# Loading the first batch's rows ahead of the first modulation weights in an AdaLN transformer layer, with zeros multiplied in the meantime

## The chip, the cores and the metric

The kernel runs on one core of a Trainium2 chip, as one program launched once. Its time is in device microseconds (us), from several executions. The profile is a record of one such execution, which has its own time.

The engines named below are PE (TensorE, matrix multiplication, with a separate row PEld for its weight loads), DVE (VectorE), ACT (ScalarE), POOL (GpSimd) and SP (SyncE, which issues most DMA transfers). SPq is SP's sequencer, on which a DMA issue takes time.

## The reference

One layer with adaptive layer norm over four batches of 512 tokens, 512 wide, all in float32:

```
mod = (silu(c) @ wmod).reshape(4, 6, 1, -1)      # c: 4 x 512, wmod: 512 x 3072
sa, ca, ga, sb, cb, gb = (mod[:, 0], ..., mod[:, 5])
ga, gb = sign-preserving max(|g|, 0.25) of each
h = layernorm(x) * (1 + ca) + sa
x = x + ga * attention(h, Wq, bq, Wk, bk, Wv, bv, Wo, bo)     # 16 heads of 128, causal
h = layernorm(x) * (1 + cb) + sb
x = x + gb * ffn(h)        # softmax router, top 2 of 8 experts, and shared experts
```

The change touches only the beginning: the first two pieces of `mod` (`sa`, called piece 0, and `ca`, called piece 1), each a product of the 4 x 512 matrix silu(c) with 512 x 512 weights, and the layer norm of the first batch's rows, which are multiplied by 1 + ca and have sa added.

## The kernel before, in words

The program is written engine by engine: each engine has its own list of instructions, run in the order written, and the lists are tied together by semaphores. No planner moves anything. Three stages follow one another: stage 1 (normalised rows, transposed; the q and k projections of all heads), stage 2 (values, scores, softmax, output projection) and stage 3 (router, experts, result). Matrix products of the stages are made of three products each, of high and low parts (`h_hi`, `h_lo` and so on), so that they keep float32 accuracy.

The very first part of stage 1 is what matters here.

- SP issues its transfers one after another on one queue (L621 to L650): `c_in`; piece 0 of the modulation weights, 1 MB, into `stage[0]` (L631, issued by the helper at L624); the four tiles of the first batch's rows, 256 KB each, into `x_in` (L633), each with its own semaphore; piece 1 of the weights into `stage[1]` (L634); five small constants, the identity and the causal mask among them (L635 to L639); the first quarter of Wq into `stage[2]` (L640); pieces 3 and 2 of the weights into `mod_early` (L641, L642); the second batch's rows (L643). Then it waits for piece 0's product (`mod_full` 1, L644) and issues raw weights and the rows of batches 2 and 3.
- `stage[0..2]` and `x_in` all are parts of the large tile `acc`, so the profile writes `acc<-wmod`, `acc<-x` and `acc<-wq` for these loads.
- ACT computes silu(c) (L1249), copies the products of pieces 0 and 1 out of PSUM into slots 2 and 3 of the tile `q_out` (L1252), and later scales transposed rows (`hidden`, L1262) and rounds them to their high part (`high`, L1269).
- PE waits for silu(c), then runs `mod_piece` (L1585 to L1592) for piece 0 and piece 1. A piece is four matmul calls over chunks of 128 rows, c = 0 to 3, with silu(c) (128 x 4) as the stationary operand and 128 x 512 weights moving. All are float32; one call appears as two MATMUL records. Then PE waits for the constants (L1607), transposes the first tile of normalised rows (L1608, in the helper at L1602), transposes the modulation rows (L1612), transposes the other three tiles, runs pieces 3 and 2 (L1617, L1618), and starts the projections of batch 0, `plain(0)` (L1626 to L1633, matmuls at L1577).
- DVE takes statistics of the four tiles as they land (`stats(0)`, L2019), POOL makes a seed for the inverse root (L952), DVE refines it and normalises the tiles (L2031 to L2036). DVE then waits for the transposed modulation rows (L2088), puts them into `modc` (L2091), scales tile 0 of the transposed rows (L2046), makes Wq's low part (L2096) and the rows' low parts (`h_low`, L2053, `hlo_ok`), and goes on with the statistics of the second batch.
- POOL rounds the first quarter of Wq (L969) as soon as it has landed.

Of the kernel before, what the change touches and what calls it, by code (L numbers as in the profile page):

```python
# [30 lines left out]
P = 128  # L31
D = 512
# [182 lines left out]
def adaln_layer(nc, x, wq, bq, wk, bk, wv, bv, wo, bo, gate_t, wexp, c_t, wmod, ident_in, causal_in,  # L215
                tri_in, coef_in, out):
    ctx = ExitStack()
    with ctx:
        def sem(name):
            return ctx.enter_context(nc.semaphore(name))  # L220

        def sbuf(scope, name, shape, dt=F32):
            return scope.enter_context(nc.sbuf_tensor(name, shape, dt))
# [15 lines left out]
        bank = [ctx.enter_context(nc.psum_tensor(f"bank{i}", [P, T], F32)) for i in range(8)]  # L239
# [22 lines left out]
        def chunks(at, dims, **sizes):  # L262
            width = int(np.prod(list(sizes.values())))
            return acc_cols[:, at:at + width].rearrange(f"p ({dims}) -> p {dims}", **sizes)

        stage = [chunks(s * DC * D, "c n", c=DC, n=D) for s in range(3)]
# [37 lines left out]
        q_out = sbuf(s1, "q_out", [P, 4, T])  # L304
# [122 lines left out]

        const_ld = sem("const_ld")
        c_ld = sem("c_ld")
        modw_ld = {0: sem("modw_ld0"), 1: sem("modw_ld1"), 3: sem("modw_ld_later"), 2: sem("modw_ld2")}  # L430
        modw_ld[4] = modw_ld[5] = modw_ld[3]
        wq0_ld = sem("wq0_ld")
        raw_ld = [sem("raw_ld0"), sem("raw_ld1")]
        x0_ld = [sem(f"x0_ld{i}") for i in range(TT)]
# [1 line left out]
        wq0_hi_ok = sem("wq0_hi_ok")  # L436
        wq0_ok = sem("wq0_ok")

        silu_c = sem("silu_c")
        mod_full = sem("mod_full")  # L440
        mod_ev = sem("mod_ev")
# [150 lines left out]
        wmod_v = wmod.rearrange("(c p) n -> p c n", p=P)  # L592
# [26 lines left out]
        def _(sp):  # L619
# [3 lines left out]
            def mod_weights(m, to):  # L623
                sp.dma_start(to, wmod_v[:, :, m * D:(m + 1) * D]).then_inc(modw_ld[m], 16)  # L624
# [3 lines left out]
                sp.dma_start(raw[i % 2], (wq_v if kind == "q" else wk_v)[:, :, pair * 2 * P:(pair + 1) * 2 * P])\  # L628
                  .then_inc(raw_ld[i % 2], 16)

            mod_weights(0, stage[0])  # L631
            for t in range(TT):
                sp.dma_start(x_in[:, t, :], x_t[:, t, :]).then_inc(x0_ld[t], 16)  # L633
            mod_weights(1, stage[1])  # L634
            sp.dma_start(ident[:, :], ident_in).then_inc(const_ld, 16)  # L635
            sp.dma_start(causal[:, :], causal_in).then_inc(const_ld, 16)
            sp.dma_start(bq_c[:, :], bq).then_inc(const_ld, 16)
# [933 lines left out]
        def _(pe):  # L1571
            def mm3(dst, terms):
# [5 lines left out]
                        k += 1  # L1578
                return ins

            pe.wait_ge(silu_c, 1)

            MOD_FREE = {3: (mod_ev, 1), 2: (modc_ok, 2), 5: reader(0, 1), 4: (s_exp, 3)}

            def mod_piece(m, w, to):  # L1585

                pe.wait_ge(modw_ld[m], {5: 32, 4: 48}.get(m, 16))
                if m in MOD_FREE:
                    pe.wait_ge(*MOD_FREE[m])
                for c in range(DC):  # L1590
                    ins = pe.matmul(bank[to][0:B, :], c_silu[:, c, :], w[:, c, :], start=(c == 0), stop=(c == DC - 1))
                ins.then_inc(mod_full, 1)  # L1592

            def transposes(b, i):
# [8 lines left out]
                ins.then_inc(tx_full, 1)  # L1603

            mod_piece(0, stage[0], 6)
            mod_piece(1, stage[1], 0)
            pe.wait_ge(const_ld, 5 * 16)  # L1607
            transposes(0, 0)  # L1608
# [6 lines left out]
            for i in range(1, TT):  # L1615
                transposes(0, i)
            mod_piece(3, mod_early[:, 0], 6)  # L1617
            mod_piece(2, mod_early[:, 1], 7)  # L1618

# [363 lines left out]
            for n in range(Z0 + 1, NJ):  # L1983
                k = n - Z0
# [6 lines left out]
        def _(dve):  # L1991
# [3 lines left out]
            def link(ins):  # L1995

                dc[0] += 1
                ins.then_inc(dchain, 1)
                dve.wait_ge(dchain, dc[0])
# [12 lines left out]
            def stats(b):  # L2012

                if b:
                    dve.wait_ge(x_ld[b - 1], 16)
                for i in range(TT):
                    if b == 0:
                        dve.wait_ge(x0_ld[i], 16)
                    ins = dve.bn_stats(stat[:, i, :], xs[b][:, i, :])  # L2019
                link(ins)  # L2020
                for i in range(TT):
                    ins = dve.bn_aggr(ln_mv[:, b, i, :], stat[:, i, :])
                link(ins)
                dve.tensor_scalar(ln_ve[:, b, :], ln_mv[:, b, :, 1], EPS, None, ALU.add).then_inc(ln_var, 1)

            def normalise(b):

                dve.wait_ge(ln_var, b + 1)
                dve.wait_ge(ln_seed, b + 1)
                seed = ln_rs0[:, b, :]  # L2030
                link(dve.tensor_tensor(nt1[:, :], seed, seed, ALU.mult))  # L2031
                link(dve.tensor_tensor(nt2[:, :], nt1[:, :], ln_ve[:, b, :], ALU.mult))
                link(dve.tensor_scalar(nt1[:, :], nt2[:, :], -0.5, 1.5, ALU.mult, ALU.add))
                link(dve.tensor_tensor(rstd[:, :], nt1[:, :], seed, ALU.mult))
                for i in range(TT):
                    dve.tensor_scalar(xs[b][:, i, :], xs[b][:, i, :], ln_mv[:, b, i, 0:1], rstd[:, i:i + 1],  # L2036
                                      ALU.subtract, ALU.mult).then_inc(xn_ok, 1)
# [43 lines left out]
            def sums_low(i):  # L2081
                s = (i + 1) % 2
                dve.wait_ge(uh_ok, 2 * i + 2)
                dve.tensor_tensor(s_w[1][s], s_raw, s_w[0][s].bitcast(F32), ALU.subtract).then_inc(ul_ok, 1)

            stats(0)
            normalise(0)
            dve.wait_ge(modt_full, 1)  # L2088
# [549 lines left out]
            for n in range(Z0, NJ - 1):  # L2638
                k = n - Z0
# [66 lines left out]
```

## Time and profile before

| what | value |
| --- | --- |
| median of 3 executions | 1536.74 us (1535.05 to 1537.42) |
| profiled execution, its own time | 1537.87 us |
| span of its record | 1535.7 us |
| mean granted TensorE clock | 0.998 |
| PE busy | 1507.5 us, 98% of the span |
| DVE, ACT, POOL busy | 988.1, 734.4, 717.1 us |
| share of PE in the chain that ended last | 86% |
| DMA | 304.05 MB, mean 198 GB/s |

The busy times are sums over the instructions of an engine, and an engine's share is its busy time over the span. The chain that ended last is followed back from the last instruction, at each step to what released it. The span is cut into 40 equal slices on the page, 38.4 us each: PE is at 7 tenths in the first slice, at 9 in all between and at 8 in the last.

### The profile page before, as it was taken

To read this page: it belongs to the slowest core of one execution; us is meant where nothing else is said; L and a number is where in the kernel's file an instruction comes from. 1 tells how busy PE (TensorE), PEld (TensorE's weight loads), DVE (VectorE), ACT (ScalarE), POOL (GpSimd) and SP (SyncE) were. 2 spreads that over 40 slices of the span, in tenths; PEclk is the share of its full clock that TensorE was granted. 3 is DMA by queue.
4 is the path that set the end of the run, shared out by engine and by line. 5 is a ranking of instruction groups with operands and counts; after the bars stand their busy time and mean duration, and the time that the engine had idled before them with its cause. 6 is when DMAs were issued, how large, how long until landed. Compare 5 with 4: busy or idle time off the path is not lost.

```text
span 1535.7 us, 29335 instructions
## 1 busy us (share of the span) xinstructions
PE 1507.5 (98%) x8844; PEld 1344.4 (88%) x8844; DVE 988.1 (64%) x2222; ACT 734.4 (48%) x1743; POOL 717.1 (47%) x767
## 2 busy tenths in 40 slices
PE   7999999999999999999999999999999999999998
PEld 3688888887999999999999999988999899999997
DVE  5977666677777777777777777774458322222268
ACT  3542222345666666666666666663332233333333
POOL 1212433346765566666566656678823211111054
PEclk9999999999999999999999999999999999999999
DMA  9336555577858486656757484745243455755566
GB/s 319 124 135 209 209 195 192 187 264 248 258 163 247 148 251 185 204 179 208 213 174 233 140 249 144 238 146 204 79 167 144 179 200 199 279 222 206 188 192 197
DMA packets 203295, 304.05 MB, mean 198 GB/s; under 512 B 80384, under 2 KB 142208, under 8 KB 196048
## 3 DMA queue, kind: packets, MB, share of 16 engines
q1 hardware_dynamic: 196096, 281.80, 54.8%
q0 software_dynamic: 5680, 18.62, 4.1%
q10 hardware_dynamic: 1440, 2.62, 0.5%
q8 instruction: 45, 0.74, 0.2%
q14 instruction: 34, 0.28, 0.1%
HBM read 187.35 MB, written 115.64 MB: 197 GB/s over the span
## 4 chain that ended last, share of the span: by engine, by line
PE 86%; DVE 4%; POOL 3%; DMA 3%; issue 2%; ACT 1%; SPq 0%; POOLq 0%; ACTq 0%; DVEq 0%
PE bank L1577 47%; PE bank L1675 17%; PE bank L1790 7%; PE bank L1742 7%; PE bank L1773 4%; PE bank L1844 2%; PE bank L1880 1%; DMA xin<-ffn_rows,slot_tokens 1%; DMA keys<-k_ring 1%; DMA ffn_rows<-h 1%; DMA acc<-wq 1%; POOL acc L1023 0%; POOL acc L1021 0%; DVE h L2629 0%; DVE h L2614 0%
## 5 line engine op out<-in xcount | busy, mean ns | idle before, releaser
L1577 PE MATMUL bank<-w,xt_hi 128*128 (+2 forms) x1136 | 281.5, 330 | 1.1 <-DMA w<-experts_lo 1.0
L1577 PEld LDWEIGHTS bank<-w,xt_hi 128*128 128x128 f32 x1136 | 196.8, 189 | 7.9 <-DMA w<-experts_lo 1.3
L1577 PE MATMUL bank<-w,xt_lo 128*128 (+2 forms) x568 | 183.6, 323 | 0.0
L1401 ACT ACTIVATE prob<-prob,row_inv 128x128 f32<-128x128 f32 (+3 forms) x256 | 137.4, 560 | 79.6 <-DVE row_inv L2243 79.4
L2363 DVE TENSOR_TENSOR ht_lo<-bank,ht_hi 128x128 fp32r<-128x128 f32 (+1 forms) x213 | 48.4, 283 | 181.7 <-ACT ht_hi L1518 181.6
L1389 ACT ACTIVATE prob<-bank,neg_max 128x128 f32<-128x128 f32 (+3 forms) x256 | 133.8, 526 | 41.3 <-DVE neg_max L2235 41.1
L1577 PE MATMUL bank<-wv_hi,h_hi 128*128 128x256 f32 x512 | 147.1, 287 | 0.0
L1577 PE MATMUL bank<-w,ht_hi 128*128 (+3 forms) x426 | 140.1, 410 | 5.2 <-DVE ht_lo L2363 4.5
L1577 PE MATMUL bank<-wv_lo,h_hi 128*128 128x256 f32 x512 | 144.7, 283 | 0.0
L1577 PE MATMUL bank<-wv_hi,h_lo 128*128 128x256 f32 x512 | 144.7, 283 | 0.0
L1201 POOL DMA_INDIRECT xin<-ffn_rows,slot_tokens x39 | 39.8, 1022 | 185.8 <-PE bank L1844 181.5
L2230 DVE TENSOR_REDUCE row_max<-bank 128x1 f32<-128x128 f32 (+3 forms) x256 | 119.8, 489 | 6.6
L986 POOL TENSOR_TENSOR ch_lo<-ch_raw,ch_hi 128x340 fp32r<-128x340 f32 x128 | 117.8, 921 | 10.3
L984 POOL CAST q_hi<-q_raw 128x512 fp32r<-128x512 f32 x62 | 69.0, 1112 | 114.9 <-PE bank L1742 109.0
L1000 POOL TENSOR_TENSOR k_ring<-acc,k_ring 128x512 fp32r<-128x512 f32 x48 | 62.1, 1307 | 120.8 <-ACT k_ring L1371 120.8
L2206 DVE TENSOR_TENSOR pt_lo<-bank,pt_hi 128x512 fp32r<-128x512 f32 (+1 forms) x192 | 106.3, 596 | 5.4 <-ACT pt_hi L1415 2.5
L1577 PEld LDWEIGHTS bank<-w,xt_lo 128*128 128x128 f32 x568 | 106.8, 188 | 0.0
L1491 ACT ACTIVATE xt_hi<-bank 128x512 fp32r<-128x512 f32 x71 | 42.5, 599 | 132.3 <-PE bank L1844 132.3
L2206 DVE TENSOR_TENSOR v_lo<-bank,v_hi 128x512 fp32r<-128x512 f32 x64 | 44.3, 692 | 94.3 <-ACT v_hi L1408 94.3
L1675 PE MATMUL bank<-t_parts,unit_hi 128*128 128x512 f32 x336 | 103.5, 389 | 0.0
L986 POOL TENSOR_TENSOR q_lo<-q_raw,q_hi 128x512 fp32r<-128x512 f32 x62 | 97.5, 1573 | 5.0
L1577 PEld LDWEIGHTS bank<-wv_lo,h_hi 128*128 128x128 f32 x512 | 97.7, 191 | 0.1
(249 smaller groups left out, 4125.8 us busy)
## 6 DMA issues: line engine op xcount, KB each, us to landing
keys<-k_ring SPq DMA_DIRECT2D x64, 512.0 KB, 3.5
ch_raw<-wexp SPq DMA_DIRECT2D x128, 170.0 KB, 3.0
experts_hi<-ch_hi SPq DMA_DIRECT2D x128, 170.0 KB, 2.6
experts_lo<-ch_lo SPq DMA_DIRECT2D x128, 170.0 KB, 2.7
w<-experts_hi SPq DMA_DIRECT2D x10, 2176.0 KB, 7.9
w<-experts_lo SPq DMA_DIRECT2D x10, 2176.0 KB, 14.6
q_transposed<-q_out SPq DMA_DIRECT2D x64, 256.0 KB, 2.1
k_even<-keys SPq DMA_DIRECT2D x16, 1024.0 KB, 5.5
```

What stands on the lines that cost most here:

```text
L984: pool.tensor_copy(hi, raw).then_inc(split_hi, 1)
L986: pool.tensor_tensor(lo, raw, hi.bitcast(F32), ALU.subtract).then_inc(done, 1)
L1000: pool.tensor_tensor(ring[e][:, 1, :], src, ring[e][:, 0, :].bitcast(F32), ALU.subtract).then_inc(kl_ok, 1)
L1389: ins = act.activation(prob[:, h, ROW_AT[r]:ROW_AT[r] + (r + 1) * P], bank[s_bank(i, first and m is n)][:, at:at + (r + 1) * P], ACT.Exp, ...
L1401: ins = act.activation(part, part, ACT.Copy, scale=row_inv[:, h, r:r + 1])
L1577: ins = pe.matmul(dst, a, m, start=(k == 0), stop=(k == last))
L1675: ins = pe.matmul(bank[to[j]][:, :], a, m, start=q == 0, stop=q == 5)
L1742: ins = pe.matmul(dst, a[:, h, r * P:w], k_both[s][:, key, h, 0:w], start=(k == 0), stop=(k == 2))
L1773: ins = pe.transpose(bank[PT_BANKS[g]][:, at + (r - k) * P:at + (r - k + 1) * P], prob[:, h, ROW_AT[r] + k * P:ROW_AT[r] + (k + 1) * P], i ...
L1790: ins = pe.matmul(bank[6 + h][:, k * P:T], a[:, k, vals], m[:, h, cols], start=(k == 0 and q == 0), stop=(g == 2 and q == 2))
L2206: dve.tensor_tensor(dst, src, hi.bitcast(F32), ALU.subtract).then_inc(done, 1)
L2230: ins = dve.tensor_reduce(row_max[:, h, r:r + 1], at_bank[:, at:at + (r + 1) * P], AX_X, ALU.max)
```

## The change

SP issues the four row tiles first, then piece 0 of the modulation weights, then piece 1 as two transfers of 512 KB, each with a semaphore of its own: chunks 0 and 1, and chunks 2 and 3. PE waits for the two halves separately, inside the loop over chunks. At its start DVE fills slot 0 of `q_out` with zeros, and PE, as its first work, multiplies those zeros by themselves four times into PSUM bank 5, whose content is not used. Slot 0 of `q_out` and bank 5 are written anew by their usual producers later.

```
-        modw_ld = {0: sem("modw_ld0"), 1: sem("modw_ld1"), 3: sem("modw_ld_later"), 2: sem("modw_ld2")}
+        modw_ld = {0: sem("modw_ld0"), 3: sem("modw_ld_later"), 2: sem("modw_ld2")}
         modw_ld[4] = modw_ld[5] = modw_ld[3]
+        mod1_ld = [sem("modw_ld1_first"), sem("modw_ld1_rest")]
...
+        idle_ok = sem("idle_tile_ok")
...
-            mod_weights(0, stage[0])
             for t in range(TT):
                 sp.dma_start(x_in[:, t, :], x_t[:, t, :]).then_inc(x0_ld[t], 16)
-            mod_weights(1, stage[1])
+            mod_weights(0, stage[0])
+            for k in range(2):
+                sp.dma_start(stage[1][:, 2 * k:2 * k + 2, :], wmod_v[:, 2 * k:2 * k + 2, D:2 * D]).then_inc(mod1_ld[k], 16)
...
+            pe.wait_ge(idle_ok, 1)
+            for _ in range(4):
+                pe.matmul(bank[5][:, :], q_out[:, 0, 0:P], q_out[:, 0, :], start=True, stop=True)
             pe.wait_ge(silu_c, 1)
...
             def mod_piece(m, w, to):
 
-                pe.wait_ge(modw_ld[m], {5: 32, 4: 48}.get(m, 16))
+                if m != 1:
+                    pe.wait_ge(modw_ld[m], {5: 32, 4: 48}.get(m, 16))
                 if m in MOD_FREE:
                     pe.wait_ge(*MOD_FREE[m])
                 for c in range(DC):
+                    if m == 1 and c % 2 == 0:
+                        pe.wait_ge(mod1_ld[c // 2], 16)
                     ins = pe.matmul(bank[to][0:B, :], c_silu[:, c, :], w[:, c, :], start=(c == 0), stop=(c == DC - 1))
                 ins.then_inc(mod_full, 1)
...
+            dve.memset(q_out[:, 0, :], 0.0).then_inc(idle_ok, 1)
             stats(0)
             normalise(0)
```

## Rows read from the trace of the kernel before

**Rows 1.** The page: engines' busy time, and the chain that ended last.

```profile
PE 1507.5 (98%) x8844; PEld 1344.4 (88%) x8844; DVE 988.1 (64%) x2222; ACT 734.4 (48%) x1743; POOL 717.1 (47%) x767
PE 86%; DVE 4%; POOL 3%; DMA 3%; issue 2%; ACT 1%; SPq 0%; POOLq 0%; ACTq 0%; DVEq 0%
```

**Rows 2.** Timeline of PE: start, length, instruction, count, idle before with its releaser.

```profile
6.71 9.43 PE L1591 MATMUL bank<-acc,c_silu 128*4 128x512 f32 x16 [6.71 <-DMA acc<-wmod]
16.06 0.66 PE L1602 MATMUL bank<-ident,acc 128*128 128x128 f32 x4
...
17.23 1.53 PE L1602 MATMUL bank<-ident,acc 128*128 128x128 f32 x12
18.69 7.03 PE L1591 MATMUL bank<-mod_early,c_silu 128*4 128x512 f32 x16
25.65 0.50 PE L1577 MATMUL bank<-h_hi,unit_hi 128*128 128x512 f32 x1
```

**Rows 3.** Timeline of PEld in the same stretch, the weight loads of pieces 0 and 1.

```profile
7.51 0.13 PEld L1591 LDWEIGHTS bank<-acc,c_silu 128*4 128x4 f32 x1 [0.72 <-issue]
8.37 0.13 PEld L1591 LDWEIGHTS bank<-acc,c_silu 128*4 128x4 f32 x1 [0.72 <-issue]
...
12.54 0.09 PEld L1591 LDWEIGHTS bank<-acc,c_silu 128*4 128x4 f32 x1 [0.34 <-issue]
...
15.11 0.09 PEld L1591 LDWEIGHTS bank<-acc,c_silu 128*4 128x4 f32 x1 [0.34 <-issue]
```

**Rows 4.** DMA issues at 1.22, 3.48, 4.01 and 7.08 us: count, size, us to landing.

```profile
acc<-wmod SPq DMA_DIRECT2D x1, 1024.0 KB, 5.3
...
acc<-x SPq DMA_DIRECT2D x2, 256.0 KB, 5.8
...
acc<-wmod SPq DMA_DIRECT2D x1, 1024.0 KB, 8.1
...
acc<-wq SPq DMA_DIRECT2D x1, 1024.0 KB, 8.3
```

**Rows 5.** Timeline of SP's issues at the start.

```profile
1.22 0.50 SPq L624 DMA_DIRECT2D acc<-wmod  x1
1.77 2.20 SPq L633 DMA_DIRECT2D acc<-x  x4
4.01 0.45 SPq L624 DMA_DIRECT2D acc<-wmod  x1
```

**Rows 6.** Windows: us, busy of PE, PEld, DVE, ACT, POOL, PEclk, DMA share, GB/s.

```profile
3.00:4.00 1.00, 0.00 (x0) 0.00 (x0) 0.00 (x0) 0.00 (x0) 0.00 (x0) 1.00 0.75 233
7.00:8.00 1.00, 1.00 (x2) 0.13 (x1) 0.70 (x2) 0.00 (x0) 0.00 (x0) 1.00 1.07 410
9.00:10.00 1.00, 1.00 (x2) 0.13 (x1) 1.00 (x2) 0.00 (x0) 0.00 (x0) 1.00 1.05 389
```

**Rows 7.** Timeline of DVE, ACT and POOL around the same work.

```profile
7.30 2.73 DVE L2019 BATCH_NORM_STATS2 stat<-acc 128x6 f32<-128x512 f32 x4 [7.30 <-DMA acc<-x]
12.76 1.92 DVE L2036 TENSOR_SCALAR acc<-acc,ln_mean_var,rstd 128x512 f32<-128x512 f32 x4
15.45 1.90 POOL L969 CAST unit_hi<-acc 128x2048 fp32r<-128x2048 f32 x1 [3.61 <-DMA acc<-wq]
16.17 0.59 ACT L1252 ACTIVATE q_out<-bank 4x512 f32<-4x512 f32 x1 [2.85 <-PE bank L1591]
17.34 0.26 DVE L2091 TENSOR_SCALAR modc<-bank 128x16 f32<-128x16 f32 x2 [2.67 <-PE bank L1612]
23.88 1.29 DVE L2053 TENSOR_TENSOR h_lo<-h_raw,h_hi 128x512 fp32r<-128x512 f32 x2 [1.22 <-ACT h_hi L1269]
```

**Rows 8.** First instructions of POOL, and a later fill by POOL.

```profile
0.72 0.10 POOL L946 MEMSET minus_half<- 128x4 f32 x1 [0.29 <-POOLq L2699]
L1136 POOL MEMSET ones<- 128x128 f32 x1 | 0.2, 206 | 0.0
```

**Rows 9.** Timeline of PE around its longest later gaps.

```profile
75.48 1.98 PE L1602 MATMUL bank<-ident,x_later 128*128 128x128 f32 x16 [1.66 <-issue]
77.53 0.39 PE L1577 MATMUL bank<-h_lo,unit_hi 128*128 128x512 f32 x1
77.77 0.39 PE L1577 MATMUL bank<-h_hi,unit_lo 128*128 128x512 f32 x1
...
1048.10 0.66 PE L1844 MATMUL bank<-ident,xin 128*128 128x128 f32 x4 [1.98 <-DMA xin<-ffn_rows]
```

## The prediction

> **What bounds the kernel now.** I read the page first. PE is busy for 98% of the span and carries 86% of the chain that ended last [rows 1]. So an edit pays only where PE stands still or runs slowly, or where it moves work off PE. The one place in the record where PE stands still for long is the start: PE's timeline shows nothing before 6.71 us, released by the first transfer of modulation weights [rows 2]. Its other gaps are at most 1.98 us [rows 9].
>
> The next view is the weight loads of that first block. There are 16 MATMUL records for the eight calls of pieces 0 and 1. The loads come 0.86 us apart at first (7.51, 8.37) and 0.43 us apart later (12.54 to 15.11 is six steps of 0.43) [rows 3]. Instruction and shape are the same, so PE ran at half speed, 1.2 GHz, after having stood idle, and rose to 2.4 GHz while it worked. The granted clock in the windows reads 1.00 in both parts [rows 6]; here the spacing tells more than that column. The last load stands at 15.11 and its matmul begins one step later, so the block ends at 15.11 + 0.43 + 0.43 = 15.96, and the transposes begin at 16.06. Of n half-speed records, 0.853n + 0.427(16 - n) = 15.96 - 6.71 = 9.25 gives n = 5.7, or 4.85 us at half speed. The slow start costs 5.7 x 0.427 = 2.4 us.
>
> The third view is the transfers. Piece 0 landed at 1.22 + 5.3 = 6.52, the fourth row tile at 3.48 + 5.8 = 9.28, piece 1 at 4.01 + 8.1 = 12.11, Wq's quarter at 7.08 + 8.3 = 15.38 [rows 4]. 1 MB takes 2.8 us between landings, and the DMA engines are full from 4 us on, at 389 to 410 GB/s [rows 6]. So in this stretch the landing time of a transfer is set by the bytes ahead of it and hardly by the moment of its issue.
>
> What follows the block is one chain: ACT's copy at 16.17, `modc` at 17.34 [rows 7], the transposes to 18.76, pieces 3 and 2 from 18.69 (16 x 0.427 = 6.83, to 25.5), the projections at 25.65 [rows 2]. The last low part of the rows, which the projections need too, ends at 23.88 + 1.29 = 25.17 [rows 7], 0.4 us before PE is free; it hangs on `modc` as well. Whatever moves the end of piece 1 moves all of this equally.
>
> **The change part by part.**
>
> *Rows first.* Piece 0 now has 1 MB of rows ahead of it. Together they are the 2 MB that had landed at 9.28 before, so I put piece 0's landing at 9.28. Bounds: it is issued at 1.22 + 2.20 + 0.05 = 3.47 [rows 5], and from there the nearest rows are 5.3 us (nothing ahead) and 8.1 us (two other MB ahead) [rows 4], which is 8.8 to 11.6. The value by bytes lies near the low end, as it should, since by 3.47 only part of one MB is still ahead. PE started 0.19 us after the landing, so 9.47 instead of 6.71: a loss of 2.76 us if nothing else changed.
>
> *Zeros.* DVE's fill has nothing before it; POOL's first instructions run at 0.72. POOL fills 128x128 in 0.21 us [rows 8], DVE passes 128x512 in 1.92 / 4, near 0.5 us [rows 7]; the fill is between these and 0.85, and I take 0.5, so PE begins at 1.3. Four float32 calls are eight records. At 0.853 us, and with the rise after 4.85 us as in the block before, they end at 1.3 + 4.85 + 2.3 x 0.427 = 7.1; never rising, at 1.3 + 6.8 = 8.1. Both lie before 9.47, so the zeros cost nothing: their cover is the wait for the weights. They would begin to cost at a fill of over 1.8 us. The fill delays DVE's statistics by nothing, since these wait for rows.
>
> *Pieces 0 and 1 at full speed.* If the clock is up and stays up over the 2.4 us from 7.1 to 9.47, the 16 records take 16 x 0.427 = 6.83 and end at 16.30. Before it was 15.96: **+0.34 us**. The bounds of the landing make it 15.8 to 18.6, so -0.1 to +2.7. The longest gaps that the record shows before work at full speed are 1.98 us and 1.66 us, and after the latter the projections come at 0.24 us a record (77.53, 77.77) [rows 9]; 2.4 us is a little beyond what the rows show. The Trainium skill (TensorE: Matmul & The Clock Gate, HAM oscillation) says that a wait for data between bursts, if it is long, puts the array back to half clock, so that the next burst starts slow again. By it the sum would be the slower rival's below; by the rows on shorter gaps it is +0.34.
>
> *Piece 1 in halves.* Its first half would land near 10.7 and its second at 12.1, by the same bytes. PE comes to it at 9.47 + 3.41 = 12.9, and to chunk 2 at 14.6. The whole of it would have been there, so the split gains 0. Its cover fails only if the stream runs 0.8 us late. It adds one issue, 0.45 us on SP [rows 5], to all that follows; but those transfers stand in a full queue, and I cost it at 0. Wq's quarter has 8.3 us between issue and landing, and the bytes before it are the same.
>
> *Rows earlier.* They land 2.7 us sooner, so statistics (7.30) and normalised tiles (12.76 to 14.7) [rows 7] move up to about 10 to 12. Their first user on PE is the transpose at 16.06, behind piece 1 in PE's list. The slack there was 1.4 us and becomes some 4 us. Gain 0. POOL's cast of Wq at 15.45 waits for its bytes and does not move. SP's wait for piece 0's product goes from about 12.7 to 12.9, with several MB still queued; cost 0.
>
> **Sum.** +2.76 (later start) - 2.42 (no slow start) = +0.34 us. On the profiled execution's own time, 1537.87 (span 1535.7 and 2.2 around it), that gives 1538.2. The median shown, 1536.74, is 1.1 below that execution, so the forecast is 1536.74 + 0.34 = **1537.1 us**.
>
> **The rivals.**
>
> *The clock falls back, or zeros never raise it (slower).* Place: the 2.4 us between the zeros and piece 0. Then pieces 0 and 1 take 9.25 us again, from 9.47 to 18.72, against 15.96: +2.76, 1539.5 us. It decides from the point at which a pause of this length costs the clock. For it: no row shows a pause as long as this followed by full speed, and none shows work on zeros. Against it: 1.66 us did no harm, and a landing at 8.8 would make the pause 1.7 us too.
>
> *The slow start was longer in other executions (faster).* Place: pieces 0 and 1 of before. If the rise usually came after 9 records and not 5.7, before would pay 1.4 us more than its record shows, and the change would take that away: 1536.74 - 1.4 + 0.34 = 1535.7 us. All 16 at half speed would be the end of it, -4.4 + 0.34. For it: the executions lie 2.4 us apart. Against it: the profiled one is the longest of the four, and more likely than not had a long slow start already. The Trainium skill (TensorE: Matmul & The Clock Gate, The HAM clock gate) says that the moment of the rise varies between runs; one record cannot show that.
>
> *The earlier rows reach the path.* If DVE's or POOL's work on the first tiles had set the transposes, 1 us or so could be won: 1536 us. Against it stands the 1.4 us of slack at 16.06 [rows 2, 7].
>
> *The change does nothing that shows, absorbed later.* Some later wait that does not hang on PE swallows the 0.34: 1536.7 us. PE's waits for transfers after the start are few and short [rows 1, 9], but such an amount is small.
>
> **How the numbers follow.** Forecast, with the landing's spread: 0.63. Clock down again: 0.14. Longer slow start before: 0.11. Earlier rows: 0.04. Absorbed: 0.08. What this kernel's measurement can tell from no change is 0.2%, 3.07 us, so faster begins at 1533.7 and slower at 1539.8. Only the slower rival comes near a bound, and with the scatter of a median of about 1 us it crosses in some four of ten cases (0.06); a landing near the high bound adds 0.03. On the fast side only the extreme of the second rival and something unseen reach 1533.7: 0.06. That leaves 0.85 for the middle. The range is from 1534.9 (faster rival, less scatter) to 1539.7 (slower rival).
>
> **What would show it.** Right: eight PE records from about 1.3 us, the first 0.85 apart and the last 0.43; a pause; LDWEIGHTS at about 9.5, every 0.43 us; last at 15.4; transposes at 16.4; first L1577 at 26.0. The fill under 0.7 us. Row tiles landed by 6.6, piece 0 at 9.3, halves near 10.7 and 12.1. Wrong: loads 0.86 apart after 9.5 (clock rival); piece 0 landing far from 9.3; the projections not starting at 25.65 plus the shift of piece 1's end; or a new gap of over 1 us after 26 us. A median more than 3 us away from 1536.7 would mean that something outside this stretch decided.

## The result: 0.2% slower, and the profile after

The changed kernel takes 1540.09 us, the median of 20 executions, against 1536.18 us for 20 of the kernel before: a ratio of 1.0022, with a 95% interval of 1.0015 to 1.0028. That is 3.4 us more (0.0022 x 1536.2), while the two medians lie 3.9 apart. The forecast was 1537.1 us, +0.34, in a range from 1534.9 to 1539.7; the median lies 0.4 above the end of that range, and the ratio applied to 1536.18 gives 1539.6, just inside it. One of the 20 executions of the changed kernel took 2492.25 us at a mean granted clock of 0.556, and the ratio leaves it out. On two later chips the same pair gave 1.0017 (1.0008 to 1.0027) and 1.0038 (1.0025 to 1.0052). The sign of the forecast was right, its size was not: what came is near the time of the slower rival (1539.5), but as the records below show only a part of it by the rival's mechanism.

The page of the changed kernel, the two lines that answer to [rows 1], shows no difference that would explain this:

```profile
PE 1510.3 (98%) x8852; PEld 1346.4 (88%) x8852; DVE 989.4 (64%) x2223; ACT 733.5 (48%) x1743; POOL 715.8 (47%) x767
...
PE 88%; DVE 5%; issue 2%; POOL 2%; DMA 1%; ACT 1%; SPq 0%; ACTq 0%; DVEq 0%; POOLq 0%
```

The timeline of PE answers to [rows 2]: start, length, instruction, count, idle before and releaser.

```profile
1.44 5.91 PE L1586 MATMUL bank<-q_out 128*128 128x512 f32 x8 [1.44 <-DVE q_out L2095]
10.89 7.03 PE L1600 MATMUL bank<-acc,c_silu 128*4 128x512 f32 x16 [3.53 <-DMA acc<-wmod]
17.84 0.66 PE L1611 MATMUL bank<-ident,acc 128*128 128x128 f32 x4
...
20.47 7.03 PE L1600 MATMUL bank<-mod_early,c_silu 128*4 128x512 f32 x16
27.43 0.50 PE L1580 MATMUL bank<-h_hi,unit_hi 128*128 128x512 f32 x1
```

The zeros run from 1.44 to 7.35, near what was worked out (1.3 to 7.1). Then PE stands for 3.5 us, not 2.4, because it can start piece 0 only at 10.89, not at 9.47. The 16 records take 7.0 us at full speed. The transposes begin at 17.84 where they began at 16.06 [rows 2], and the projections at 27.43, not 25.65: a shift of 1.78 us in both places.

Where the 1.4 us come from is in the windows, which answer to [rows 6] (last three columns: granted clock, DMA share, GB/s). First three of the kernel before, then those of the changed kernel:

```profile
4.00:5.00 1.00, 0.00 (x0) 0.00 (x0) 0.00 (x0) 0.00 (x0) 0.00 (x0) 1.00 1.05 403
5.00:6.00 1.00, 0.00 (x0) 0.00 (x0) 0.00 (x0) 0.00 (x0) 0.00 (x0) 1.00 1.05 391
6.00:7.00 1.00, 0.29 (x1) 0.12 (x2) 0.00 (x0) 0.00 (x0) 0.00 (x0) 1.00 1.04 399
```

```profile
4.00:5.00 1.00, 1.00 (x2) 0.34 (x1) 0.28 (x1) 0.00 (x0) 0.00 (x0) 1.00 1.04 348
5.00:6.00 1.00, 1.00 (x3) 0.46 (x2) 0.80 (x2) 0.00 (x0) 0.00 (x0) 1.00 1.07 309
6.00:7.00 1.00, 1.00 (x4) 0.28 (x2) 0.99 (x2) 0.00 (x0) 0.00 (x0) 1.00 0.75 219
7.00:8.00 1.00, 0.35 (x1) 0.00 (x0) 0.71 (x2) 0.00 (x0) 0.00 (x0) 1.00 0.94 334
8.00:9.00 1.00, 0.00 (x0) 0.00 (x0) 0.55 (x5) 0.00 (x0) 0.24 (x1) 1.00 1.06 406
```

From 4 to 8 us the stream moves 348, 309, 219 and 334 GB/s; in the kernel before it moved 403, 391, 399 and 410 (the last in [rows 6]). That is 1.21 MB in place of 1.60, and the missing 0.39 MB are 1.0 us at 400 GB/s. From 8 us on the stream is as fast as before. The rest is in what had moved by the landing: 2.64 MB between 1 and 10.79 us here, 2.40 MB between 1 and 9.28 us before, so some 0.24 MB more of other transfers, or 0.6 us, had gone alongside. The transfers' own lines, piece 0 issued at 3.19 and the halves of piece 1 at 3.67 and 4.21, answer to [rows 4]:

```profile
acc<-wmod SPq DMA_DIRECT2D x1, 1024.0 KB, 7.6
...
acc<-wmod SPq DMA_DIRECT2D x1, 512.0 KB, 8.4
...
acc<-wmod SPq DMA_DIRECT2D x1, 512.0 KB, 9.3
```

So piece 0 landed at 3.19 + 7.6 = 10.79, and the second half of piece 1 near 13.5; PE came to it at 10.89 + 6 x 0.86 = 16.0 (six calls at 0.86 us each, two records a call). The split is idle, as forecast. Wq's quarter, costed at nothing, did move: POOL's cast of it begins at 16.91 in place of 15.45, still 8.6 us before the projections' start.

This record has the clock up over the whole pause. Its execution took 1537.45 us, one of the six that lie between 1536.99 and 1537.77; thirteen more lie between 1539.0 and 1542.5. So the record is of one of the shorter executions, and the main question for the experiments was what the others do.

### The profile page after: what moved, and what is told of

The parts are those of the page before. It is cut to its first block, busy times and chain, and to the rows that moved or that the text cites. A ratio compares the mean times of both kernels' runs of the same rounds, so it can differ in the third digit from the quotient of the medians.

```text
span 1535.3 us, 29353 instructions
## 1 busy us (share of the span) xinstructions
PE 1510.3 (98%) x8852; PEld 1346.4 (88%) x8852; DVE 989.4 (64%) x2223; ACT 733.5 (48%) x1743; POOL 715.8 (47%) x767
## 4 chain that ended last, share of the span: by engine, by line
PE 88%; DVE 5%; issue 2%; POOL 2%; DMA 1%; ACT 1%; SPq 0%; ACTq 0%; DVEq 0%; POOLq 0%
PE bank L1580 49%; PE bank L1684 17%; PE bank L1799 7%; PE bank L1751 7%; PE bank L1782 4%; PE bank L1853 2%; PE bank L1889 1%; DMA ffn_rows<-h 1%; DMA acc<-wq 1%; POOL acc L1026 0%; POOL acc L1024 0%; DVE h L2639 0%; DVE h L2624 0%; DVE row_max L2240 0%; DVE pt_lo L2216 0%
```

## Experiments

Ratios are to the kernel before on the same chip, with 95% intervals. The chips differ: before took 1541.29, 1536.11 and 1539.16 us in the three sets.

**The changed kernel again.** No edit.

> The changed kernel once more, for more executions and a second record. Theory (late landing and a pause that mostly costs the clock): the recorded execution of before had pieces 0 and 1 end at 15.96 us, that of the changed kernel at about 17.75, a shift of 1.8; in that record the clock stayed up over a pause of 3.5 us, and its time, 1537.45, is among the lowest of twenty. The others lie at 1539 to 1542.5, so the theory wants two groups 2 to 3 us apart, near 1537.4 and 1540.3, and if the record falls on a slow one, LDWEIGHTS of piece 0 must come 0.86 us apart again. Rival (the loss comes from later work, where the transfers of stage 3 land): one spread around 1539.5, and 0.43 us spacing in any record.

Ratio 1.0017 (1.0008 to 1.0027), median 1543.83. The record fell on an execution in which the clock went down. Windows of it:

```profile
9.40:9.80 0.40, 0.00 (x0) 0.00 (x0) 0.27 (x2) 0.00 (x0) 0.00 (x0) 1.00 1.06 399
9.80:10.20 0.40, 0.00 (x0) 0.00 (x0) 0.33 (x3) 0.00 (x0) 0.00 (x0) 0.58 1.05 389
10.20:10.60 0.40, 0.34 (x1) 0.12 (x2) 0.36 (x2) 0.00 (x0) 0.00 (x0) 0.50 1.01 374
12.60:13.00 0.40, 0.40 (x2) 0.13 (x1) 0.00 (x0) 0.00 (x0) 0.00 (x0) 0.50 1.05 375
13.00:13.40 0.40, 0.40 (x1) 0.00 (x0) 0.00 (x0) 0.00 (x0) 0.00 (x0) 0.65 1.04 379
```

and its weight loads and transposes:

```profile
11.07 0.13 PEld L1600 LDWEIGHTS bank<-acc,c_silu 128*4 128x4 f32 x1 [0.72 <-issue]
11.92 0.13 PEld L1600 LDWEIGHTS bank<-acc,c_silu 128*4 128x4 f32 x1 [0.72 <-issue]
...
13.89 0.09 PEld L1600 LDWEIGHTS bank<-acc,c_silu 128*4 128x4 f32 x1 [0.34 <-issue]
...
18.70 0.66 PE L1611 MATMUL bank<-ident,acc 128*128 128x128 f32 x4
```

PE had stopped at 7.62. The granted clock went from 1.00 to 0.50 at about 9.9 (0.58 is the mean of that window) and came back at about 13.3 (0.65 in the last window), and the loads stand 0.85 apart in between. Here the granted clock shows directly what in [rows 3] only the spacing told. The 11 executions spread evenly from 1541.6 to 1547.7, without two clear groups, so the theory's claim of two groups is not borne out there.

The clock fell in later places too, and this the theory had left out. From the same record, PE's start after a pause near the end of stage 3, and the windows around it:

```profile
1481.61 0.95 PE L1580 MATMUL bank<-w,xt_hi 128*128 128x352 f32 x2 [3.06 <-DVE xt_lo L2216]
```

```profile
1480.00:1482.00 2.00, 0.39 (x1) 0.39 (x2) 1.14 (x2) 1.77 (x3) 0.00 (x0) 0.75 0.60 160
1482.00:1484.00 2.00, 2.00 (x8) 2.00 (x8) 1.90 (x4) 0.05 (x1) 0.00 (x0) 0.50 0.21 78
```

The record of before has no such pause and 1.00 in these windows. A pause of 2.9 to 3.1 us released there by DVE is in seven of the eight records of this chip and of the last one, that of zeros in the order of before among them, and in none of the six from the other chips. So the rows in front are not needed for it, but it adds microseconds to a record that the start does not explain.

**Without the zeros.** The fill, the four calls and their semaphore are taken out of the changed kernel.

```
-            pe.wait_ge(idle_ok, 1)
-            for _ in range(4):
-                pe.matmul(bank[5][:, :], q_out[:, 0, 0:P], q_out[:, 0, :], start=True, stop=True)
...
-            dve.memset(q_out[:, 0, :], 0.0).then_inc(idle_ok, 1)
```

> The changed kernel without the zeros (no fill, no four calls). Theory of the clock: pieces 0 and 1 always start slowly, 9.2 us for 16 records in place of 6.8, so the time is that of the upper group, 1540 us or some 4 us over before, in all executions. Question beside it: the stream of transfers moved 309 and 219 GB/s in the windows 5 to 6 and 6 to 7 us, against 391 and 399 before. If the zeros (PE reading, DVE filling) slow it, piece 0 lands near 9.3 and not 10.8 here, and the time is about 1538.7; if the rows in front are the cause, it lands near 10.8 again. Rival (later work): no difference to the changed kernel, within 1 us.

Ratio 1.0020 (1.0011 to 1.0029), median 1544.7, 0.9 above the changed kernel on that chip. Piece 0 is there at 10.08, and the windows 4 to 5 and 5 to 6 move 197 and 348 GB/s. So neither PE's reading of zeros nor DVE's fill slows the stream; it is the rows in front. Pieces 0 and 1 take 9.93 us, and the transposes begin at 19.95, the latest of all. The pieces in its timeline of PE:

```profile
10.08 9.93 PE L1596 MATMUL bank<-acc,c_silu 128*4 128x512 f32 x16 [10.08 <-DMA acc<-wmod]
```

**The zeros in the order of before.** Three calls, nothing else changed.

```
+            pe.wait_ge(idle_ok, 1)
+            for _ in range(3):
+                pe.matmul(bank[5][:, :], q_out[:, 0, 0:P], q_out[:, 0, :], start=True, stop=True)
             pe.wait_ge(silu_c, 1)
...
+            dve.memset(q_out[:, 0, :], 0.0).then_inc(idle_ok, 1)
             stats(0)
```

> The kernel before with its own order of transfers and piece 1 whole, but with the zeros, three calls in place of four, so that they end near 6.6 us, when piece 0 lands. Theory of the clock: piece 0 runs at full speed from 6.7 to 10.1, then PE waits for piece 1, which lands at 12.1, and ends it at 15.7; gain 0.3 us only, since the bytes of piece 1 take the place of the slow start: 1536.0 us. Rival (the slow start is worth its 2.4 us by itself): 1533.8 us.

Ratio 0.9994 (0.9985 to 1.0003). The timeline of PE:

```profile
7.22 3.59 PE L1595 MATMUL bank<-acc,c_silu 128*4 128x512 f32 x8 [1.03 <-DMA acc<-wmod]
12.63 3.60 PE L1595 MATMUL bank<-acc,c_silu 128*4 128x512 f32 x8 [1.82 <-DMA acc<-wmod]
16.16 0.66 PE L1606 MATMUL bank<-ident,acc 128*128 128x128 f32 x4
```

Piece 0 runs at full speed, and PE then waits 1.8 us for piece 1. The transposes begin at 16.16, as in the kernel before. The slow start had stood in the shadow of piece 1's weights: taking it away alone wins nothing in this record, and the rival (2.4 us of gain) lies just outside the interval, which ends at 2.3 us.

**Longer zeros**, twice. Eight calls in place of four.

```
-            for _ in range(4):
+            for _ in range(8):
```

> The changed kernel with eight calls on zeros in place of four, 16 records, so that PE has no pause of over 1 us before piece 0 lands. They end near 10.8 us or, with a late rise of the clock, up to 1 us later. Theory of the clock: all executions fall in the lower group, 1537.5 to 1538 us, 2 to 3 us below the changed kernel's median; over before there remains the later landing, 1.3 to 2 us. Rival (later work): the same median as the changed kernel, near 1540.

> Eight calls on zeros again, for more executions: on the first chip it came out only 0.4 us below the changed kernel, with both medians uncertain by about 1 us, where the theory of the clock wants 1.5 (a fallen clock cost 1.5 us of the 8.5 us that pieces 0 and 1 took in the second record of the changed kernel). Theory: 1.0007 to 1.0012 of before, and 1 to 2 us below the changed kernel. Rival (the fallen clock is given back later, or the executions of the changed kernel rarely have it): within 0.5 us of the changed kernel again.

Ratios 1.0010 (1.0001 to 1.0019) and 1.0021 (1.0009 to 1.0032). Both records have the clock up through the pieces, with the transposes at 17.23 and 17.76 against 18.70 and 18.89 for the changed kernel on the same chips. The medians are 0.4 and 2.7 us below the changed kernel's, 1543.40 against 1543.83 and 1541.94 against 1544.68. The records show the clock's part; the times alone would not separate it, as the intervals overlap. The first set had also promised one group only, and its 12 executions spread from 1540.7 to 1545.6. So a spread of this kind is no sign of the clock at the start.

**The rows as one transfer.** One transfer of 1 MB in place of four.

```
-            for t in range(TT):
-                sp.dma_start(x_in[:, t, :], x_t[:, t, :]).then_inc(x0_ld[t], 16)
+            sp.dma_start(x_in[:, :, :], x_t[:, 0:TT, :]).then_inc(x0_ld[0], 16)
...
-                        dve.wait_ge(x0_ld[i], 16)
+                        dve.wait_ge(x0_ld[0], 16)
```

> The changed kernel with the first batch's rows as one transfer of 1 MB in place of four of 256 KB; DVE's statistics wait for the whole. In four records with the four row tiles in front, piece 0's weights reached PE at 10.05 to 10.9 us, against the 9.3 that equal bytes would give, while the stream moved only 200 to 310 GB/s in one or two of the windows between 4 and 7 us. If the four small transfers at the head of the queue cause that, piece 0 is there at about 9.4, pieces 0 and 1 end at 16.3 with the clock up, and the time is 1 us below the changed kernel's. If it is the rows themselves or the start of the queue in any order, it is there at 10 to 10.9 again, and the time stays at 1.002 of before.

Ratio 1.0007 (0.9998 to 1.0016). The windows of it:

```profile
4.00:5.00 1.00, 1.00 (x2) 0.34 (x1) 0.00 (x0) 0.00 (x0) 0.00 (x0) 1.00 1.06 408
5.00:6.00 1.00, 1.00 (x3) 0.46 (x2) 0.00 (x0) 0.00 (x0) 0.00 (x0) 1.00 1.04 383
6.00:7.00 1.00, 1.00 (x4) 0.33 (x2) 0.04 (x1) 0.00 (x0) 0.00 (x0) 1.00 1.05 408
...
9.00:10.00 1.00, 0.22 (x1) 0.12 (x2) 0.93 (x6) 0.00 (x0) 0.00 (x0) 0.72 1.05 387
10.00:11.00 1.00, 1.00 (x2) 0.13 (x1) 0.05 (x1) 0.00 (x0) 0.79 (x1) 0.50 1.04 385
```

The slow windows are gone, and piece 0 is there at 9.78. So it is the splitting of the rows into four transfers that makes the stream sag, not the megabyte of rows as such; the last version below, with one transfer too, has no slow window either. What it is about the four is not shown by this run: with one, piece 0 is also issued sooner, at 1.77 in place of 3.19. Its landing, 9.67 here and 9.47 in that other record, lies among the 9.23 to 9.79 at which 2 MB, piece 0 and the rows, were there in five records with piece 0 whole in front; the 9.28 of the kernel before is at the early end of these. With the four row tiles in front it is 9.99 to 10.79, in six records. Yet this record loses the clock, over a pause of 2.38 us, very nearly the pause that the prediction had reckoned with.

**Piece 0 in quarters.** The order of before, three calls on zeros, and the weights of piece 0 as four transfers. PE's wait for the zeros uses another semaphore of DVE's, as in the versions with pieces 3 and 2 in halves. The core of the edit, in which `PARTS` holds the number of transfers for each piece:

```
+        PARTS = {0: 4, 1: 1, 3: 1, 2: 1}
...
+                if m in PARTS:
+                    w = DC // PARTS[m]
+                    for k in range(PARTS[m]):
+                        sp.dma_start(to[:, w * k:w * k + w, :],
+                                     wmod_v[:, w * k:w * k + w, m * D:(m + 1) * D]).then_inc(part_ld[m][k], 16)
...
                 for c in range(DC):
+                    if m in PARTS and c % (DC // PARTS[m]) == 0:
+                        pe.wait_ge(part_ld[m][c // (DC // PARTS[m])], 16)
```

> The order of before with three calls on zeros, and piece 0's weights as four transfers of 256 KB at the head of the queue, each waited for apart. It is the counterpart to rows_one_transfer: if small transfers at the head slow the stream, the last quarter lands 0.7 to 1.5 us after the 6.5 to 7.1 of the whole piece, and the rows, piece 1 and Wq's quarter follow as much later (Wq's cast at 16.3 or more, not 15.5 to 16.0). If it is the rows, nothing moves. PE ends piece 0 near 8 us but waits for piece 1 until 12.1 to 12.6 either way, so the time is that of zeros_order_before, 0.999 to 1.000 of before, and up to 1.5 us more in the first case.

Ratio 1.0012 (1.0003 to 1.0021). The windows from 4 to 7 move 356, 340 and 326 GB/s. The record of zeros in the order of before, with the whole piece in front, has 354, 356 and 412 there, and that of before 403, 391 and 399; piece 1 is there at 12.50, within the usual 12.1 to 12.6. From 4 to 8 us that is 1.42 MB, where the seven records with one transfer of 1 MB in front have 1.53 to 1.60 and the six with the row tiles 1.21 to 1.44; but the 2 MB are there at 9.61, as with one transfer in front. So small transfers of weights in front may slow the stream too, but they cost the landing little, and on this the result is open. It does settle one thing: the first five issues are at the same moments as in the changed kernel (1.23 to 3.19), so the time of the issues on SP alone does not explain the late landing there. The loss in the record has another cause, which was not expected: PE is done with piece 0 at 9.6, stands for 2.9 us, and loses the clock in that pause. Piece 1 takes 4.97 us in place of 3.60, and the transposes begin at 17.41. Here PE finished early, had a longer pause in front of it, and paid for it.

**The split where it can work.** The order of before, three calls on zeros, piece 1 in halves: `PARTS = {0: 1, 1: 2, 3: 1, 2: 1}`.

> The order of before with three calls on zeros and piece 1's weights in two halves. This gives the split something to do: PE is ready for piece 1 at 10.1 to 10.8. Theory (behind the slow start stand the bytes): the first half lands near 10.9, the second at 12.2 to 12.6, piece 1 ends near 14.3 in place of 16.0; but pieces 3 and 2 follow, whose weights land at 18.0 and 20.8, so that the projections start near 25.1 in place of 25.65: 0.5 us of gain, 0.9995 of before. Rival (the end of piece 1 passes down the chain whole): projections at 24.0 and 1.7 us of gain.

Ratio 0.9994 (0.9985 to 1.0003). Transposes at 14.17; piece 3 waits for its weights until 18.21, and the projections start at 25.16, as the theory said. Yet the start of stage 2 is 1.6 us earlier, not 0.5 (table below): the theory had the wrong engine as the last one. DVE's timeline points to the right one, first before, then here:

```profile
25.09 2.46 DVE L2019 BATCH_NORM_STATS2 stat<-x_later 128x6 f32<-128x512 f32 x4
...
21.98 1.29 DVE L2068 TENSOR_TENSOR h_lo<-h_raw,h_hi 128x512 fp32r<-128x512 f32 x2 [1.14 <-ACT h_hi L1278]
23.53 2.47 DVE L2034 BATCH_NORM_STATS2 stat<-x_later 128x6 f32<-128x512 f32 x4 [0.26 <-DMA x_later<-x]
```

The statistics of the second batch began at 25.09 before, now at 23.53, and there they wait for their rows. PE then stands waiting for DVE's work on those rows, before and here:

```profile
62.15 1.06 PE L1602 MATMUL bank<-ident,x_later 128*128 128x128 f32 x8 [1.11 <-DVE h_raw L2046]
```

```profile
60.61 1.06 PE L1617 MATMUL bank<-ident,x_later 128*128 128x128 f32 x8 [1.11 <-DVE h_raw L2061]
```

That is 1.54 us earlier, as much as the statistics (1.56) and three times as much as the projections (0.49). So what counts for the rest of stage 1 is DVE's list, not the moment at which PE starts the projections.

**Pieces 3 and 2 in halves too.** `PARTS = {0: 1, 1: 2, 3: 2, 2: 2}`; on two chips.

> As zeros_split_1, with pieces 3 and 2 in halves as well, each half waited for apart (the zeros' wait uses another semaphore, which changes nothing else). Theory: PE follows the bytes of pieces 3 and 2 and ends them near 22.7, the low parts of the rows then set the start of the projections, near 23.6 to 24 in place of 25.65: a gain of 1.7 to 2 us, ratio near 0.9988. Rival (more small transfers slow the stream as they seem to at the head): the halves land a microsecond late and the gain is under 0.7 us.

> The version that was the fastest, again on another chip: 0.9985 to 0.9993 of before, or 1.2 to 2.2 us, and 4 to 5 us below the changed kernel. If the first result was scatter, it comes out at 0.9995 to 1.0005.

Ratios 0.9989 (0.9980 to 0.9998) and 0.9993 (0.9983 to 1.0002): 1.7 and 1.1 us below the kernel before (0.0011 and 0.0007 of its time), and on the second chip 7.3 us below the changed kernel by medians. The timeline of PE in the first:

```profile
10.93 3.60 PE L1605 MATMUL bank<-acc,c_silu 128*4 128x512 f32 x8 [0.38 <-DMA acc<-wmod]
14.46 0.66 PE L1616 MATMUL bank<-ident,acc 128*128 128x128 f32 x4
...
17.13 7.03 PE L1605 MATMUL bank<-mod_early,c_silu 128*4 128x512 f32 x16
24.08 0.50 PE L1585 MATMUL bank<-h_hi,unit_hi 128*128 128x512 f32 x1
```

The projections start at 24.08 and the statistics at 23.81. The halves of pieces 3 and 2 bring the projections 1.1 us forward, but nothing beyond the previous version for the start of stage 2, which fits DVE being last. It has the lowest ratios here, by an amount at the edge of what can be measured: one interval excludes no change, the other just includes it.

**The changed kernel a third time.**

> The changed kernel again, beside the two that mend it, on one chip. Where the records stand: pauses of PE of 2.4, 2.6 and 2.9 us cost the clock, one of 3.5 us did not, so the theory holds both outcomes possible for this kernel and wants 1.0015 to 1.0025 of before. In its record the clock is down between 9 and 13 us (two of three chances) or not.

Ratio 1.0038 (1.0025 to 1.0052), from only 6 executions. The clock fell at about 10.3, just after PE had resumed at 10.23 from a pause of 2.39 us. The ratio lies above what was expected. This record has the late pause as well, 2.94 us with the clock down behind it, and one of 3.65 us at 1052, where the kernel before has 1.98.

**Both terms mended.** The rows in one transfer and eight calls on zeros.

> Both terms that the prediction had wrong are taken away: the rows in one transfer, so that the stream is not slowed, and eight calls on zeros, so that PE does not pause. Theory: piece 0 is there at 9.7, pieces 0 and 1 end at 16.7, 0.7 us after those of before, and the time is 1.0003 to 1.0007 of before. Rival (something else in rows first costs 2 to 3 us, DVE's later start of the statistics among it): 1.0015 or more.

Ratio 1.0011 (1.0001 to 1.0021). Eight calls end at 10.5 and so are too many for weights that landed at 9.47 (issued at 1.77, 7.7 us to landing); the record has PE busy throughout, pieces 0 and 1 from 10.44, and the transposes at 17.40. That is 1.34 us over the kernel before, some 0.9 of it from the surplus of zeros. The theory wanted 1.0003 to 1.0007 and the rival 1.0015 or more; the ratio lies between them, and the interval excludes neither.

**All records in one table.** Start of the transposes (just behind the end of piece 1) and of stage 2 (the first matmul on `k_even`), in us. The latter is read from rows like these two, before and changed, in which it is the first number of the stretch behind the durations:

```profile
L1742 PE MATMUL bank<-k_even,q_hi x256: 220/333/404, 353.9 to 996.8; 128*128 128x128 f32 x32, 128*128 128x256 f32 x32, 128*128 128x384 f32 x32, 128*128 128x512 f32 x32
```

```profile
L1751 PE MATMUL bank<-k_even,q_hi x256: 220/333/404, 355.6 to 997.8; 128*128 128x128 f32 x32, 128*128 128x256 f32 x32, 128*128 128x384 f32 x32, 128*128 128x512 f32 x32
```

| kernel | longest pause ahead of a piece, clock | transposes | stage 2 | difference | ratio |
| --- | --- | --- | --- | --- | --- |
| before | none | 16.06 | 353.9 | 337.8 | 1 |
| changed, first record | 3.53, held | 17.84 | 355.6 | 337.8 | 1.0022 |
| changed, second | 2.64, fell | 18.70 | 356.4 | 337.7 | 1.0017 |
| changed, third | 2.39, fell | 18.89 | 356.6 | 337.7 | 1.0038 |
| without zeros | slow start | 19.95 | 357.7 | 337.8 | 1.0020 |
| rows in one transfer | 2.38, fell | 18.24 | 356.0 | 337.8 | 1.0007 |
| long zeros | 0.30, held | 17.23 | 355.0 | 337.8 | 1.0010 |
| long zeros, again | none | 17.76 | 355.5 | 337.7 | 1.0021 |
| one transfer, long zeros | none | 17.40 | 355.1 | 337.7 | 1.0011 |
| zeros, order of before | 1.82, held | 16.16 | 354.0 | 337.8 | 0.9994 |
| piece 0 in quarters | 2.90, fell | 17.41 | 355.2 | 337.8 | 1.0012 |
| piece 1 in halves | 1.34, held | 14.17 | 352.3 | 338.1 | 0.9994 |
| pieces 1, 3, 2 in halves | 0.40, held | 14.46 | 352.5 | 338.0 | 0.9989 |
| the same, again | 0.38, held | 14.31 | 352.4 | 338.1 | 0.9993 |

A microsecond at the end of piece 1 is a microsecond at the start of stage 2, some 338 us later, to 0.1 us wherever piece 1 ends later than before; of the 1.6 to 1.9 us by which it ends earlier in the last three, 0.2 to 0.3 are lost on the way. Behind that point stages 2 and 3 scatter by one to several microseconds between executions.

## Why the prediction was wrong in size

**Piece 0's landing: wrong by 0.6 to 1.4 us.** The step was "the 2 MB that had landed at 9.28", with the landing set by bytes. The rows of before show the rate of small transfers only behind a whole megabyte. With four row tiles of 256 KB at the head of the queue the stream sagged, and piece 0 was at PE at 10.89, 10.26, 10.23, 10.28 and, without zeros, 10.08, not at 9.47. With one transfer it came at 9.78, so by that one record 0.3 to 1.1 us are due to the four. The other 0.3 are within the half microsecond by which the landing of 2 MB scatters where nothing sags (9.23 to 9.79): 9.28 was an early value. These values lie inside the bounds that the prediction gave, 8.8 to 11.6, but the value was taken from the side of equal bytes.

**The clock over the pause: wrong.** The forecast rested on 1.66 and 1.98 us without harm [rows 9], and stretched that to 2.4. The second of these was misread: the rows show only the four transposes right behind that pause. In the windows of the kernel before (third column from the right) the clock falls at about 1049.2 (0.61 is the mean of that window), 1.1 us after PE resumed at 1048.10:

```profile
1048.00:1049.00 1.00, 0.90 (x6) 0.72 (x7) 1.00 (x4) 0.15 (x1) 1.00 (x2) 1.00 0.95 393
1049.00:1050.00 1.00, 1.00 (x4) 0.84 (x3) 0.55 (x2) 1.00 (x2) 0.92 (x2) 0.61 0.81 344
1050.00:1051.00 1.00, 1.00 (x4) 0.74 (x3) 0.17 (x1) 0.85 (x2) 1.00 (x2) 0.50 1.07 231
...
1053.00:1054.00 1.00, 1.00 (x8) 1.00 (x7) 0.14 (x1) 0.00 (x0) 0.98 (x2) 1.00 1.02 395
```

So the rows do not show a pause of 1.98 us without harm. Ahead of the pieces, pauses of 2.38, 2.39, 2.64 and 2.90 us all cost the clock, 1.82 did not, and one of 3.53 did not either. In stage 3 the second record of long zeros has two more, of 2.92 and 2.90 us, with the clock at 1.00 through both. So no length of pause divides the cases here. The rule of the Trainium skill that the prediction had weighed (TensorE: Matmul & The Clock Gate, HAM oscillation), that a long wait for data puts the array back to half clock, named a danger that was real. Of the pauses over 2 us ahead of the pieces, the trace agrees in four records and disagrees in the one with the longest. A fallen clock cost 1.5 us in the second record of the changed kernel (8.51 against 7.03 for the 16 records), 1.7 in the third (8.72), not the 2.4 us of the rival. In the second record the clock was down already when PE resumed at 10.26 and came back at about 13.3, within the fourth of the 16 records, 3.0 us later and sooner than the 4.85 us of work that it took in the kernel before.

**The sum.** Start 3.5 to 4.2 us later in place of 2.76, and 2.4 us of slow start saved, or 0.9 where the clock falls. The records of the changed kernel give +1.78, +2.64 and +2.83 us at the transposes. Their mean of 2.4 is 0.16% of the time, against the measured 0.22%, 0.17% and 0.38%. The remainder, about 1 us at the first chip and 3 at the last, is explained in part at most. Later falls of the clock and the pauses beside them are one source: over the 35, 33 and 30 executions of the kernel before the time rises by about 1 us for each 0.001 that the mean granted clock is lower, and the third set has 0.9958 for the changed kernel against 0.9983 for before, the second 0.9964 against 0.9973. No run shows whether the change has a part in those later falls.

**Right:** the zeros' time and that the wait covers them (1.44 to 7.35); the fill (0.48 us); the split, idle behind the slow order; the earlier rows, worth nothing; the shift passed on whole. For the last the table is the proof; but the reason given, that PE ends its pieces just as the low parts of the rows are ready, was half of it: where the two were pulled apart, DVE's list decided. That the sign came out right is partly luck: +0.34 was the difference of two terms of 2.4 and 2.8 us, the first was saved in full only where the clock held, and the second was too small in every record.

**The rival "longer slow start before"** has no support. If the kernel before usually paid 1.4 us more than its record shows, every version would look better in time than in its record. Piece 1 in halves and the two runs with pieces 1, 3 and 2 in halves reach stage 2 by 1.6, 1.4 and 1.5 us earlier than that record, and took 0.9, 1.7 and 1.1 us less. These intervals are about 1.4 us wide to either side, so a smaller excess stays possible.

## What to carry to other kernels

A slow start costs only what is not covered by the next transfer: look when the data of the following step land, and mend both together, as the zeros with piece 1 in halves did. Work that has only to keep the clock must reach up to the data it bridges to, for a pause left behind it can undo it. When transfers are reordered, do not take the rate of small ones from the middle of a full queue; put the large one at the head, or try it. And a row that shows work right behind a pause does not show that the clock held: read the granted clock of the windows for some microseconds behind it.

## What the runs showed of the hardware

- Four transfers of 256 KB at the head of a queue: in each of the six records with the row tiles in front, at least one window between 4 and 6 us at 197 to 309 GB/s, against 354 or more in those windows in all seven records with 1 MB in front, and 340 and 356 with four quarters of weights. The busy share of the DMA engines mostly falls with the rate (0.54 at 197, 0.75 at 219), but not always: it reads 1.07 in one window at 309 GB/s and 1.05 in another at 311, so a full share does not vouch for a full stream.
- The granted clock of PE went from 1.00 to 0.50 in pauses of 2.38, 2.64 and 2.90 us and just behind one of 2.39, and 1.1 us after PE had resumed from one of 1.98; it stayed at 1.00 over pauses of 2.90, 2.92 and 3.53 us. Pauses of this size can cost the clock or not. Multiplying zeros raised the clock as other work does: eight records of zeros took 5.91 us, where all at half speed would take 6.8, and piece 0 behind them ran at full speed.
- In the first microseconds of a record the column of the granted clock reads 1.00 while matmuls are spaced as at half speed; after a fall later on it reads 0.50 at the same spacing. At the start, go by the spacing.
